# One layer's normalised activations: the high half made by ScalarE in every layer, the low half by GpSimd a turn later

## What is computed

```python
for l in range(depth):
    residual = x
    h = _layernorm(x, gamma[l], beta[l])
    qkv = h @ w_qkv[l]
    q, k, v = jnp.split(qkv, 3, axis=-1)
    q = jax.nn.softmax(q, axis=1)
    k = jax.nn.softmax(k, axis=2)
    context = jnp.einsum('bic,bjc->bij', k, v)
    out = jnp.einsum('bic,bij->bjc', q, context)
    out = out @ w_out[l] + b_out[l]
    x = out + residual
```

## Time and profile before

| what | value |
|---|---|
| median of 3 runs | 1413.93 us (1412.33 to 1418.26) |
| the profiled execution, its time | 1416.26 us |
| its span (first to last instruction) | 1414.5 us |
| busy over the span: PE, DVE, ACT, POOL | 1266.3, 1031.7, 833.7, 944.1 us |
| the attention turns | from some 125 us to 935 us |

### The profile page before, as it was taken

How to read it: one execution, slowest core, us unless ns; L and a number is a source line. 1 busy time by engine, 2 the same in 40 slices (tenths; PEclk the granted TensorE clock), 3 DMA queues, 4 the chain that set the end, 5 groups by cost and what they waited for, 6 DMA issues and landing times. The chain is left out here.

```text
span 1414.5 us, 36691 instructions
## 1 busy us (share of the span) xinstructions
PE 1266.3 (90%) x10994; PEld 1056.3 (75%) x10995; DVE 1031.7 (73%) x2647; ACT 833.7 (59%) x2297; POOL 944.1 (67%) x950
## 2 busy tenths in 40 slices
PE   4415889999999999999999999986999999999996
PEld 3414778888888888888888888754555888888885
DVE  2346899999999999999888899873555545454543
ACT  2204678788888888887887787744542333333331
POOL 2057787899889988988998999647552243434343
PEclk8757999999999999999999999998999999999998
DMA  9943745644544553225323755514435444454441
GB/s 338 369 131 91 156 129 137 171 109 124 138 100 111 131 137 77 67 59 137 68 60 67 157 103 93 96 36 128 122 109 140 73 60 68 62 70 61 68 61 14
DMA packets 349078, 156.66 MB, mean 111 GB/s; under 512 B 279856, under 2 KB 333392, under 8 KB 349008
## 3 DMA queue, kind: packets, MB, share of 16 engines
q1 hardware_dynamic: 315168, 116.92, 34.4%
q0 software_dynamic: 20112, 25.32, 10.3%
q10 hardware_dynamic: 13728, 13.63, 2.7%
HBM read 44.62 MB, written 43.16 MB: 62 GB/s over the span
## 5 line engine op out<-in xcount | busy, mean ns | idle before, releaser
L855 PE MATMUL bank<-hT,Wc 128*128 128x256 f16 x2304 | 285.7, 274 | 43.8 <-DMA hT<-hhl 30.4
L855 PEld LDWEIGHTS bank<-hT,Wc 128*128 128x128 f16 x2304 | 226.6, 98 | 71.8 <-issue 44.2
L810 POOL DMA_INDIRECT out_rows<-h0b,payin x78 | 121.6, 1558 | 209.0 <-DVE h0b L1697 177.0
L956 PE MATMUL bank<-xTg,Wall 128*128 128x256 f16 x1872 | 211.0, 273 | 1.3 <-DMA xTg<-slot_x 1.3
L956 PEld LDWEIGHTS bank<-xTg,Wall 128*128 x1872 | 182.8, 98 | 23.5 <-issue 1.9
L1230 ACT ACTIVATE silu<-bank 128x512 f32<-128x512 f32 x110 | 65.5, 595 | 183.7 <-PE bank L956 135.2
L1367 DVE SCALAR_TENSOR_TENSOR gT<-bank,silu 128x512 f32<-128x512 f32 x110 | 75.9, 691 | 111.3 <-ACT silu L1230 103.2
L855 PE MATMUL bank<-Wc,MT 128*128 128x256 f16 x1152 | 142.7, 274 | 12.7 <-DVE MT L1458 12.7
L687 POOL TENSOR_TENSOR h0b<-h0b,rows 128x512 f32<-128x512 f32 x80 | 102.3, 1279 | 72.5 <-issue 38.6
L855 PE MATMUL bank<-khl,eqT 128*128 128x256 f16 x1152 | 141.3, 272 | 5.2 <-DVE khl L1470 0.2
L855 PE MATMUL bank<-Wc,hT 128*128 128x256 f16 x1152 | 143.9, 276 | 0.0
(11 more groups left out here) (179 smaller groups left out, 2647.8 us busy)
## 6 DMA issues: line engine op xcount, KB each, us to landing
Wall<-in_L_tok_W SPq DMA_DIRECT2D x25, 512.0 KB, 8.4
emb<-Wall ACTq DMA_DIRECT2D x25, 512.0 KB, 10.1
Wall<-in_L_ffn_ew SPq DMA_DIRECT2D x24, 512.0 KB, 4.0
Wc<-Wn SPq DMA_DIRECT2D x40, 128.0 KB, 2.3
Wst<-in_L_attn_w_qkv SPq DMA_DIRECT2D x12, 384.0 KB
h_rows<-Wall SPq DMA_DIRECT2D x8, 512.0 KB
X<-h_rows POOLq DMA_DIRECT2D x8, 512.0 KB, 6.7
out_rows<-X SPq DMA_DIRECT2D x8, 512.0 KB
```

The source lines that it names most:

```text
L810: pool.indirect_dma_start(out=out_rows, out_offset=bass.IndirectOffsetOnAxis(ap=got(j % PAYS, w, 0, i32), axis=0), in_=yout[j % 2][:, w, : ...
L855: last = mm(to, lhs(a, k, o), moving, start=(i == 0 and k == 0), stop=(i == 2 and k == 1))
L956: last = mm(to, cols(a, e, 2 * k + w, (2 * half + c) * P, P), moving, start=(n_ == 0), stop=(n_ == 5))
```

## The change

ScalarE's copy of `hf` into the high half (L1187) is now made for every item, in ScalarE's turn t for item t+4. GpSimd no longer makes the rounded sum (L692), and its subtraction (L665) for item t+4 stands at the start of turn t, where it waits for ScalarE's signal; in turn t-1 it stood between L709 and L716. All other engines' instructions are the same.

```diff
-                if early(t + 4) and t >= 0:
+                if have(t + 4) and not (isinstance(t, int) and t < 0):
                     pool.wait_ge(s_hh, t + 5)
+                    pool.sem_inc(s_passed, 1)
                     low_half(t + 4, p)
...
                     pool.wait_ge(s_hg, u + 1)
-                    wait(pool, s_hT[1 - p], landed(u - 2))
+                    wait(pool, s_h, u)
                     pool.sem_inc(s_passed, 1)
-                    pool.tensor_tensor(hhl[1 - p][:, 0, :, :], xn[:, :, :], row(1), ALU.add)
                     pool.tensor_tensor(hf[:, :, :], xn[:, :, :], row(1), ALU.add).then_inc(s_hf, 1)
...
-                if have(u) and not early(u):
-                    pool.wait_ge(s_hf, u + 1)
-                    low_half(u, 1 - p)
...
                 i = t + 5 if isinstance(t, int) and t < -1 else t + 4
-                if early(i) and t != -1:
+                if have(i) and not (isinstance(t, int) and t == -1):
+                    q = i % 2 if isinstance(i, int) else p
                     act.wait_ge(s_hf, i + 1)
-                    if i >= 2:
-                        act.wait_ge(s_hT[i % 2], landed(i - 2))
-                    A(hhl[i % 2][:, 0, :, :], hf[:, :, :], ACT.Copy).then_inc(s_hh, 1)
+                    if not (isinstance(i, int) and i < 2):
+                        act.wait_ge(s_hT[q], landed(i - 2))
+                    act.sem_inc(s_passed, 1)
+                    A(hhl[q][:, 0, :, :], hf[:, :, :], ACT.Copy).then_inc(s_hh, 1)
```

## The result

The changed kernel takes 1403.35 us (median of 8 runs, 1399.40 to 1408.61), the kernel before on the same chip 1412.80 (8 runs, 1406.70 to 1418.26). The ratio is 0.9939, 95% interval 0.9919 to 0.9958: 0.6% less, 8.6 us of 1413. The forecast was 1404.0 us, 0.7% less.

The account below looks back on a forecast made before the run. VectorE was taken to bound chunk turns, GpSimd plain ones, above TensorE's 7.87 us floor; -6.4 - 2.0 - 1.3 - 1.4 + 1.2 = -9.9 us gave 1404.0 us, range 1400 to 1408.

Parts of the forecast that it names:

- The term: 24 turns with CUT and chunk: 0.36 us saved each, 8.6, less losses of 1.2 and 1.0, giving -6.4 us.
- L665 meets L1317: GpSimd's subtraction overlapping VectorE's chunk instruction: up to 0.15 us lost in 12 turns, 1.2 us with other turns' small shares.
- The wait for `hf`: ScalarE ready for its copy slightly before GpSimd's sum is signalled, in CUT and chunk turns: 0.04 a turn, 1.0 us.
- the second rival: ScalarE becomes the bound in CUT and chunk turns, saving only 0.15 us a turn: 1407 us, chance 0.20.
- the norm stretches L656 to 1.00: Reading of contention in CUT turns: VectorE's norm lengthens GpSimd's weight piece to 1.00 us, itself growing from 0.73 to 1.09.
- less than a whole instruction of waiting: Claim that the trace shows VectorE and GpSimd contending for SBUF, but less than the exclusive lock's rule says.
- The first rival: Slower: GpSimd's subtraction meets VectorE's chunk instruction and norm in chunk turns, 0.61 us each, +18.5: 1432 us, chance 0.09.
- ScalarE's room as the sum of its waits: CUT and chunk pairs: 1.17 us free after shorter norms, two copies take 1.00, fitting by 0.17; more room elsewhere.
- has more than that until VectorE takes it: In turns with a chunk alone, ScalarE's PR would start 0.1 to 0.2 us later, within its slack; change 0.
- the CUT turns alone and the plain ones: Turns without a chunk fall towards TensorE's 7.87 us: 8 x 0.25, -2.0, from 8.17, and -1.3 from 8.02.
- The last chunk turns: from 8.34 to the 8.10 of the others: The last six turns with a chunk fall to the others' length: 6 x 0.24, -1.4 us.
- turn 91: ScalarE's copy waits for item 95's sum from GpSimd: +1.5 us, less 0.3 for the norm in turn 90, +1.2.

Follow-up runs that it names:

- same_turn: Changed kernel with ScalarE's copy kept but GpSimd's subtraction in its old place, waiting there for the copy: 1401.76 us, ratio 0.9979 to the kernel before.
- cut_at_norm: Changed kernel with GpSimd's weight piece L656 of each even looped CUT turn moved to the next turn, beside the norm: 1407.09 us, ratio 0.9962 to the kernel before.

## Why the prediction was right, and where not

**Right: L656 beside the norm was what VectorE, and with it the CUT and chunk turns, lost.** VectorE is not the bound over the whole turn, since it waits some 0.5 us in each, but it is on the stretch from the chunk to PR. The norm is 0.73 us in all these turns, and L656 put back returns 1.08 and nearly half of the gain in half of the turns. The term was -6.4 and came out at -6.8.

**Right by size, wrong by name: the two losses in it.** "L665 meets L1317", -1.2, did not happen: all 16 chunk instructions read take 0.68 us. The wait for `hf`, -1.0, is not shown: the copy's 0.6 us in eight turns have no releaser in the view, and the longer of the two came well after `hf` was whole. That 2.2 was taken off and 1.8 is missing is luck. What the runs show of it: ScalarE's CUT order holds 0.8 us of the 1.8 (8.18 to 8.15 a turn), which is the second rival's mechanism at a small size, and these turns then stand 0.03 above those with a chunk alone, which themselves rose from 8.10 to 8.12. What makes up that last part was not tested.

**Wrong reading: "the norm stretches L656 to 1.00", and a price by share.** L656 started at 445.36, inside L1317, and ended 0.53 us after it; in the turns with CUT alone, which have no chunk instruction, it keeps its 0.66 us (685.06) although it stretches the norm beside it to 1.08 (685.12). It was the chunk and not the norm that stretched it. So "less than a whole instruction of waiting" was no sign against the lock: the norm came when L656 had 0.6 us to go, and waited for all of it. The first rival's 0.61 by the share of lengths is 0.84 by the places of the ends.

**Wrong by reasoning: ScalarE's room as the sum of its waits.** That sum gave 0.17 us a pair of CUT and chunk turns and "more room" elsewhere. One more activation behind khl costs 0.34 us a turn where ScalarE waits 1.07 us a turn, and 0.02 us ahead of vT. Room ahead of the wait for MT can't be spent behind it. That the first copy cost nearly nothing in chunk turns (+0.44 us in 24) is so because PR had the slack that the prediction named ("has more than that until VectorE takes it"), not because ScalarE had idle time.

**Right: the CUT turns alone and the plain ones** fall to TensorE's floor, 7.88 us; -3.6 against -3.3. The allowance for loop edges (0.25 taken where the floor gives 0.30) was not needed: the eight turns with CUT alone take 63.00 us with TensorE busy for all of it.

**The step that failed: "The last chunk turns: from 8.34 to the 8.10 of the others".** They went to 8.40. What held them at 8.34 was not what the change takes away: it was the norm beside GpSimd's DMA issue (1.21 us in three turns), which the prediction does not name. It counted L665 as moved past the wait for `xn`, and it was moved past that DMA issue too, which the section on the kernel names. In three turns this put L665 onto the chunk, 1.27 us instead of 0.68, which is the first rival's mechanism, in turns where nobody had looked for it. With L665 ahead of the issue the turns take 8.22, so -0.8 was to be had and +0.4 came; the 8.10 of the others was not reached there either, for the norm beside the issue is then still 0.96 (828.22 in same_turn). Two of the prediction's own signs of being wrong stand here: a longer chunk instruction, and chunk turns above 8.10.

**Right: turn 91,** +1.6 against +1.2, by the wait that was named: 1.87 us of the copy for `hf`.

**Not forecast:** turns 1 to 9 differ by +1.7 us between these two traces; over all eleven they take 85.2 to 88.7. Most of it lies in turns 2 and 3. In turn 2 VectorE waits for the landing of a piece of the embedding (`Wall<-emb`), 3.45 us before and 3.73 after, TensorE stands idle for 4.3 and 4.6 us, and its granted clock then falls. Windows of turn 3, in the changed kernel and in cut_at_norm, which has the same instructions in these turns:

```profile
159.46:169.85 10.39, 10.39 (x86) 8.81 (x85) 8.76 (x22) 7.05 (x24) 7.28 (x8) 0.89 0.57 152
157.34:165.44 8.10, 7.99 (x72) 6.98 (x72) 7.92 (x22) 6.44 (x21) 5.72 (x7) 1.00 0.64 174
```

With the clock at 0.89, TensorE is busy for the whole turn; at 1.00 the turn is 8.10. The kernel before has 0.87 in turn 2 and 1.00 in turn 3 (8.30 us). Since two traces with the same instructions differ by more than the 1.7, I put nothing of it down to the change. But seven of the eight traces with the changed kernel's code in these turns have the slow turn 3, and none of the other three, so that a part in it is not ruled out.

**The first rival, slower,** did not come, but its mechanism did, when made: 0.8 us a turn instead of the 0.61 by which it was priced; the kernel that makes it happen in all turns of the loops stands 2.8%, 39 us, above the kernel before, where the rival had +18.5.

## What to carry to other kernels

When VectorE and GpSimd work on SBUF at the same time, the later of the two can wait for nearly the whole of the other, so look at which one ends last and not at how long they are. Taking an instruction away may be worth less than where it lets the next ones fall, and the two halves of an edit can be worth 0 and +13 us alone and -7 together. So read which instructions lie side by side at the bound engine's last steps, and keep the other engine out of there. An engine's idle time is not one purse: ask ahead of which of its waits the new work stands, for only waits behind it and ahead of its next consumer pay for it. And when a step moves to another turn, list every instruction that it passes in the turns written out by hand too, DMA issues included.

## What the runs showed that I had not expected

Right behind the DMA issue L723 (1.35 us long), GpSimd's subtraction is recorded from 0.50 us before the issue's end and ends 1.19 to 1.20 us after it, where alone it takes 1.15: it starts its work only when the issue is over, and a longer record is no sign of contention. And the same norm loses 0.36 us to L656 (0.68 us alone) and 0.84 to L665 (1.16 us alone), which looked out of proportion; in both cases its first instruction ends 0.15 us after theirs, and theirs was itself held by the chunk instruction before it.
